# Adding gathered node rows to edge rows: by VectorE from a gather buffer, or in place by an accumulating gather

## The reference, cut to what matters

```python
def _L3_gnn_ref(x, edge_index, edge_attr, W1, b1, W2, b2, gamma, beta):
    src, dst = (edge_index[0], edge_index[1])
    msg = jax.nn.relu(x[src] + edge_attr)                 # 21250 x 512
    agg = jax.ops.segment_sum(msg, dst, num_segments=x.shape[0])
    h = x + agg
    h = jax.nn.relu(h @ W1 + b1) @ W2 + b2
    h = x + h
    mean = h.mean(axis=0)
    var = h.var(axis=0)
    return (h - mean) * jax.lax.rsqrt(var + BN_EPS) * gamma + beta
```

## Time and profile before

| | |
|---|---|
| median of 3 runs | 764.68 us |
| profiled execution, span | 770.4 us |
| first gather issued to last gather issued | 381.8 to 689.8 us |
| busy: PE / DVE / ACT / POOL | 83% / 52% / 34% / 50% |
| gathers (L471), POOL busy | 217.3 us in 168 |
| VectorE add (L978), busy | 96.3 us in 42 |
| DMA queue of the gathers | 44.05 MB, 18.0% of 16 engines |
| queue of SP's loads and stores | 58.59 MB, 21.4% of 16 engines |

### The profile page before, as it was taken

The page is one execution under the profiler, slowest core; times in us unless marked ns, Lnnn a source line. Parts: engine busy times, 40 slices in busy tenths (PEclk is TensorE's granted clock), DMA queues, the critical chain, the costliest instruction groups (busy, mean ns, idle before and its releaser), DMA issues.

```text
span 770.4 us, 9550 instructions
## 1 busy us (share of the span) xinstructions
PE 635.7 (83%) x2854; PEld 411.5 (53%) x2854; DVE 397.7 (52%) x765; ACT 262.4 (34%) x434; POOL 383.3 (50%) x401
## 2 busy tenths in 40 slices
PE   2597886998988988999886877988898978798963
PEld 1343335997888827988521333433354433345962
DVE  3798882766648492117443333434443434432767
ACT  1354442112463154111532423244333332343135
POOL 7388888201012038300177777777776777760000
PEclk9699997999999998999899899998999989999985
DMA  7600000000002000024568788877888788650003
GB/s 225 183 2 0 1 0 4 0 0 1 1 1 94 17 1 1 0 71 162 192 234 272 251 309 290 280 267 272 311 297 307 253 284 279 207 149 0 1 0 134
DMA packets 30332, 103.09 MB, mean 134 GB/s; under 512 B 6559, under 2 KB 7201, under 8 KB 24986
## 3 DMA queue, kind: packets, MB, share of 16 engines
q1 hardware_dynamic: 16858, 58.59, 21.4%
q0 software_dynamic: 13440, 44.05, 18.0%
HBM read 97.51 MB, written 5.12 MB: 133 GB/s over the span
## 4 chain that ended last, share of the span: by engine, by line
PE 33%; POOL 31%; issue 17%; DVE 9%; ACT 5%; DMA 3%; POOLq 1%; ACTq 0%; SPq 0%; DVEq 0%
POOL xg L471 25%; PE ps L1171 15%; PE ps L1196 8%; PE ps L1369 3%; POOL hot_lo L395 3%; POOL idx L467 2%; DVE stats L871 2%; DVE xn L891 2%; ACT countsT L563 2%; PE ps L1131 1%; DMA xg<-x_dram,idx 1%; PE ps L1146 1%; DMA row_src_i<-in_src_dram 1%; PE ps L1332 1%; PE ps L1311 1%
## 5 line engine op out<-in xcount | busy, mean ns | idle before, releaser
L471 POOL DMA_INDIRECT xg<-x_dram,idx x168 | 217.3, 1293 | 73.4 <-issue 40.2
L1311 PE MATMUL ps<-ea,hot_w 128*38 128x512 f32 x336 | 170.2, 654 | 50.6 <-ACT ea L636 50.5
L978 DVE TENSOR_TENSOR ea<-ea,xg 128x2048 f32<-128x2048 f32 x42 | 96.3, 2292 | 180.6 <-DMA xg<-x_dram,idx 180.6
L636 ACT ACTIVATE ea<-ea 128x2048 f32<-128x2048 f32 x42 | 80.2, 1910 | 186.9 <-DVE ea L978 186.9
L1311 PEld LDWEIGHTS ps<-ea,hot_w 128*38 128x38 f32 x336 | 38.3, 124 | 151.4 <-issue 95.2
L395 POOL TENSOR_SCALAR hot_lo<-iota_n,lo_col 128x128 bf16<-128x128 f16 x84 | 56.5, 683 | 8.6 <-POOL lo_col L391 8.6
L1131 PE MATMUL ps<-hot_code,hot_lo 128*128 128x380 bf16 x168 | 38.1, 353 | 20.3 <-POOL hot_lo L395 20.2
L777 DVE TENSOR_SCALAR hot_code<-iota_n,codeT 128x380 bf16<-128x380 f16 x168 | 52.6, 373 | 4.2 <-issue 3.8
L1332 PE MATMUL ps<-zg,w_s 128*128 128x114 f32 x448 | 53.6, 278 | 0.4 <-ACT zg L652 0.4
L467 POOL COPY idx<-srcT_i 128x4 int32 (+1 forms) x42 | 19.2, 456 | 66.9 <-issue 66.7
L1332 PEld LDWEIGHTS ps<-zg,w_s 128*128 128x128 f32 x448 | 51.1, 192 | 1.1 <-ACT zg L652 0.5
(11 more groups left out here) (193 smaller groups left out, 1092.7 us busy)
## 6 DMA issues: line engine op xcount, KB each, us to landing
ea<-in_edge_attr_dram SPq DMA_DIRECT2D x41, 1024.0 KB, 6.9
w_s<-in_L_gnn_W_dram SPq DMA_DIRECT2D x5, 1024.0 KB, 11.6
xg<-x_dram,idx POOLq DMA_INDIRECT x168, 5.3
xn<-in_x_dram SPq DMA_DIRECT2D x3, 768.0 KB, 13.1
x_dram<-xn SPq DMA_DIRECT2D x9, 256.0 KB
out_dram<-xn SPq DMA_DIRECT2D x9, 256.0 KB
w_s<-in_L_gnn_W_dram SPq DMA_DIRECT2D x2, 512.0 KB, 9.0
b_b<-in_L_gnn_b_dram SPq DMA_DIRECT2D x3, 256.0 KB, 5.6
```

The costliest lines, as they stand in the source:

```text
L471: pool.indirect_dma_start(out=xg[:, slot, r, :], out_offset=None, in_=x3_dram[:, :], in_offset=bass.IndirectOffsetOnAxis(ap=idx4[:, slot, ...
L636: act.activation(ea[:, s, :, :], ea[:, s, :, :], ACT.Relu).then_inc(relu_done, 1)
L978: dve.tensor_tensor(ea[:, s, :, :], ea[:, s, :, :], xg[:, slot, :, :], ALU.add).then_inc(add_done, 1)
L1311: ins = pe.matmul(ps[0:W, 4 + s % 2, :], hot_w[:, s, r, :], ea[:, s, r, :], start=(r == 0), stop=(r == TPG - 1))
```

## The change

VectorE's add and the gather buffer's use in the stream go. POOL waits until a group's edge rows have landed (`ea_loaded[s]`) and issues the four gathers with `compute_op=ALU.add` straight onto `ea[:, s, r, :]`. The index is taken from `srcT_i` itself: the gathers are written out for all 42 groups, so the group number is a constant, and the copy into `idx4` with its wait goes. ScalarE's relu waits for `xg_loaded[s]` in place of `add_done`. POOL's wait on the group three before goes with the buffer; `ea` stays a ring of six. In the irregular branch nothing changes.

```diff
-        xg_loaded = [sem(f"xg_loaded{i}") for i in range(XRING)]
-        idx_staged, idx_seen = sem("idx_staged"), sem("idx_seen")
-        add_done, relu_done, win_ready = sem("add_done"), sem("relu_done"), sem("win_ready")
+        xg_loaded = [sem(f"xg_loaded{i}") for i in range(RING)]
+        idx_seen = sem("idx_seen")
+        relu_done, win_ready = sem("relu_done"), sem("win_ready")
...
-            def gather(it, s):
-                g, slot = RING * it + s, s % XRING
-                if not (isinstance(g, int) and g < XRING):
-                    pool.wait_ge(add_done, g - XRING + 1)
-                pool.tensor_copy(idx4[:, slot, :], srcT_i[:, bass.ds(g, 1), :].rearrange("p a b -> p (a b)")).then_inc(idx_staged, 1)
-                pool.wait_ge(idx_staged, g + 1)
-                pool.sem_inc(idx_seen, 1)
+            def gather(g):
+                s = g % RING
+                pool.wait_ge(ea_loaded[s], 16 * (g // RING + 1) + 16 * (g == NG - 1 and LAST_R > 0))
                 for r in range(TPG):
-                    pool.indirect_dma_start(out=xg[:, slot, r, :], out_offset=None, in_=x3_dram[:, :],
-                                            in_offset=bass.IndirectOffsetOnAxis(ap=idx4[:, slot, r:r + 1], axis=0)).then_inc(xg_loaded[slot], 16)
-
-            for s in range(RING):
-                gather(0, s)
-            with pool.Fori(1, ITERS) as it:
-                for s in range(RING):
-                    gather(it, s)
+                    pool.indirect_dma_start(out=ea[:, s, r, :], out_offset=None, in_=x3_dram[:, :],
+                                            in_offset=bass.IndirectOffsetOnAxis(ap=srcT_i[:, g, r:r + 1], axis=0),
+                                            compute_op=ALU.add).then_inc(xg_loaded[s], 16)
+
+            for g in range(NG):
+                gather(g)
...
             def rectify(it, s):
                 g = RING * it + s
-                act.wait_ge(add_done, g + 1)
+                act.wait_ge(xg_loaded[s], 16 * TPG * it + 16 * TPG)
                 act.activation(ea[:, s, :, :], ea[:, s, :, :], ACT.Relu).then_inc(relu_done, 1)
...
-            def add_rows(it, s):
-
-                g, slot = RING * it + s, s % XRING
-                dve.wait_ge(xg_loaded[slot], it * (16 * TPG * RING // XRING) + 16 * TPG * (s // XRING + 1))
-
-                dve.wait_ge(ea_loaded[s], it * 16 + 16 * (1 + (isinstance(it, int) and g == NG - 1 and LAST_R > 0)))
-                dve.tensor_tensor(ea[:, s, :, :], ea[:, s, :, :], xg[:, slot, :, :], ALU.add).then_inc(add_done, 1)
+            def hot_rows(it, s):
+
+                g = RING * it + s
```

More of the change, by code:

```diff
@@ L440, in _ @@
                 pool.tensor_tensor(xn[0:rows(j), j, :], xn[0:rows(j), j, :], b2_b[0:rows(j), :], ALU.add).then_inc(xb_ready[2], 1)
+            pool.wait_ge(idx_ready, 1)
             pool.wait_ge(x3_stored, 16 * NT)
@@ L1009, in stream @@
                 for s in range(RING):
-                    add_rows(it, s)
+                    hot_rows(it, s)
                     if s % JOIN == 0 and not (isinstance(it, int) and it == 0):
```

## The result

The changed kernel takes 778.27 us (median of 4 runs, 776.39 to 778.36) against 764.42 us for the kernel before (median of 4): ratio 1.018, 95% interval 1.014 to 1.022. It is 13.9 us slower. The forecast was slower too, but by 76 us, and 778 lies in the range only because the range reached down to the case on the other side.

The account below looks back on a forecast made before the run. POOL was taken to bound the stream at 7.38 us per group. The DMA engines, with an extra read, would become the bound: +78 less 2.3 for the last add, 770.4 + 76 = 846, less 5.7: 841 us; range 728 to 915.

Parts of the forecast that it names:

- the case on the other side: Stream: the gather's extra read is free and POOL is freed, so the kernel gets faster, 720 to 738 us; 20%.
- What bounds the kernel now: Stream: POOL sets the period of 7.38 us per group, 5.71 undisturbed and the rest stalls beside VectorE's add.
- What is added: Accumulating gathers: one extra read pass per group on the DMA engines, 2.85 to 3.26 us, 120 to 137 us more; 55%.
- 8.7 to 9.7 us per group: Stream: the forecast period of the DMA engines, with gathers, edge loads and the extra read added up.
- The rule on two reads: Accumulating gathers: the DMA's add is free but two source reads share one read ring, 1.93 times a copy, 6.3 us per group.
- Descriptors: POOL's gather issues: three descriptors per row for two, 1.42 us per issue, 6.9 per group, 742 us with free reads; 5%.
- POOL has slack either way: Stream: POOL's demand falls from 7.38 to 5.0 us per group, 210 us in all, so its stalls don't change the sum.
- Half hidden: Accumulating gathers: the extra read costs about 1 to 1.5 us per group, 765 to 795 us; 10%.
- Three passes: Accumulating gathers: reading, adding and writing each cost a gather's price, 9.78 us per group, 973 us; 10%.
- The read costs nothing: Stream: the extra read rides along free and POOL is freed, 720 to 738 us, 728 at the middle; 20%.
- The 2.3 us of the last add: Last group: landing, add, relu and scatter follow one another, so dropping VectorE's add saves 2.3 us once.
- What would show it: Signs listed for the changed kernel's profile: DMA share above 0.9, issues at 0.95 us, period near 9.2 us, slower edge loads.

Follow-up runs that it names:

- written: The kernel before with gathers written out and the index copy gone, still into the gather buffer with VectorE's one long add: 731.71 us, ratio 0.960.
- tiny_add: The kernel before with VectorE's add cut to one feature of 512 per row, all waits and the index copy kept: 710.28 us, ratio 0.932.
- direct_acc: The changed kernel with one direct accumulating DMA of 1 MB in 8 KB rows per group in place of the four gathers: 764.51 us, ratio 0.999.
- inplace_plain: The changed kernel with plain gathers for accumulating ones, so node rows overwrite edge rows and the addition is left out: 705.66 us, ratio 0.927.
- half_edges: The changed kernel with only half of the edge rows reloaded for groups 6 to 40, POOL's work the same: 770.76 us, ratio 1.010.

## Why the prediction was wrong

*What bounds the kernel now*: right, and more so than written. POOL's period, and in it the index copy (0.68 us per group: `written`, 31 us for 28) and the stalls by VectorE's add. That the add stalls the gathers' issues was read from two pairs of rows and is now shown by `tiny_add`. The Trainium skill, "SBUF — State Buffer", "Who interferes with whom", infers that an add of this kind spares descriptor writing. From that I worked out 753 us for `tiny_add`, and it stands at 710: I had taken a gather's issue for descriptor writing and nothing else. The same section says that such an add contends with a POOL instruction that reads SBUF. The traces agree with both halves if a gather's issue, which takes its indices from SBUF, counts as such an instruction: direct DMAs beside the same kind of instruction took 0.536 us each, unstalled, and a gather 2.99.

*What is added: "one extra pass over 1.049 MB, priced ... 2.85 us to 3.26 us"*: this is the step that failed, with the sum built on it, "At full use of all 16 the stream lasts 367 us (+57), at the densest share seen, 0.94, 409 us (+99)". The mechanism held: the addition makes the DMA engines the bound, and `direct_acc` shows it without POOL. The size did not. I turned the share of each queue into a price per MB and added the prices, as if an engine served one packet at a time. Shares reach 74.0% + 34.9% in the changed kernel, 112.6% for one queue alone, and `inplace_plain` runs at a share of 0.99 without being held by the DMA engines. A packet's time in the share thus includes time that it spends beside other packets. My 8.7 to 9.7 us per group are 7.67 measured, and 7.44 in `direct_acc`. One pass of 1.049 MB cost a third of 7.67, 2.56 us, where I had 2.85 to 3.26; the two plain passes, 6.11 in my sum, fit into the 5.6 us per group of `inplace_plain`; and the division by 0.94 came on top. So the stream grew by 11 us in the traces and not by 57 to 99. Bytes read over a rate of 410 to 423 GB/s would have given it; my own window of 345 GB/s was a hint at a lower figure and not a limit, since POOL set the pace there.

*The rule on two reads* (the Trainium skill, "Collectives: The Full Stack", "The bandwidth ceiling: the fold count and why AG ≠ RS ≠ AR") fits as a mechanism. Its ratio of 1.93 compares with 1.9 here, 387 GB/s of plain gathers alone against 205 of accumulating ones alone. By shares (18.0% and 31.5%) the factor is only 1.75, 1.76 with the spans. On the stream it does not apply, because plain transfers were not at their limit.

*The rivals.* "Descriptors" (5%) guessed 1.42 us per issue for a measured 1.545, and I treated it as an alternative to the DMA bound. It holds together with it: POOL at 7.4 and the DMA engines at 7.67 are two limits within 4%. Either alone cancels the whole gain (770.76 us in `half_edges`, 764.51 in `direct_acc`). My sentence that POOL has slack either way was wrong by the same 0.6 us per issue. "Half hidden" (10%, 765 to 795 us) is where the result fell by number, and its 7.5 to 8.1 us per group is right by luck of the same mispriced pass. "Three passes" (10%) named packets of two rows broken into single ones. That happened, 144 packets for 80, and cost little: `direct_acc`, with a fourth of the packets for the same bytes, is 3% faster per group. "The read costs nothing" was wrong in its condition, but its prize was too small as well: without the addition the kernel takes 706 us, not 728, since neither TensorE's 6.39 us nor the DMA engines' 6.11 us was a floor. Both go down to about 5.6 when POOL does: in `inplace_plain` POOL issued 42 groups from 376.0 to 611.3.

*The 2.3 us of the last add* can't be told apart: the end of the stream grew by 7.5 us in all.

*What would show it*: a share above 0.9 and relus waiting on DMA came true, though the share proves little, as `half_edges` shows. TensorE was busy 80% (95.96 us of 120) and not 65 to 70%, the period 7.67 us and not 9.2, the gathers' queue at 245 us of 16 engines and not 270. Three signs failed: issues at 0.95 us, POOL idle on edge loads, and edge loads landing in 10 us or more (7.9). "Issues of 1.4 us" was listed as a sign against my case; it came true beside it.

## What to carry to other kernels

Moving an add into the DMA is not free: here each accumulated byte cost about what two plain ones do, and each issue 1.6 times its time, so price it in bytes and in issue time before counting what the compute engine saves. When a long two-input VectorE instruction stands beside indirect DMAs issued by POOL, look for issues that end just after it, and cut the instruction into shorter ones first: here three lines gave 5%, and 7.4% with the gathers written out. Don't add up shares of DMA queues, and don't take the durations of an engine that waits at a lower clock for its floor.

## What the runs showed of the hardware that was not expected

- Cutting one 2.29 us VectorE add into four (2.5 us in all) let the gathers' issues in between: beside it they took up to 3.0 us, and 1.1 to 1.4 in the timeline after.
- A 128x2048 VectorE instruction with both inputs in SBUF stretched an indirect issue on POOL to 2.99 us, while direct issues inside it kept their 0.536 us.
- An accumulating DMA has 144 packets per 128 rows of 2 KB where a plain one has 80, and POOL needs 1.6 times as long to issue it, indirect (1.545 for 0.947 us) or direct (0.862 for 0.536).
- Accumulating gathers alone moved 205 GB/s where plain ones alone moved 387. With two reads counted per accumulated byte, the DMA engines read 410 to 423 GB/s in total while they accumulate.
- The busy shares of two queues can sum to 1.09, and that of one alone can reach 1.13.
- TensorE was granted 1.00 of its clock from 420 to 540 us in the versions in which it is busy all the time, and 0.94 in the changed kernel with 95.96 busy us of 120.
